# One DMA transpose per batch in place of four TensorE transposes in a gated attention and expert block on one Trainium2 core

## The reference

```python
scores = einsum('bhqd,bhkd->bhqk', heads(layernorm(x) @ Wq.T), heads(ctx @ Wk.T)) + mask
probs = softmax(scores, axis=-1)
att = merge(einsum('bhqk,bhkd->bhqd', probs, heads(ctx @ Wv.T))) @ Wo.T
x = x + tanh(g_xattn) * att
xf = layernorm(x)
w, idx = top_k(softmax(xf @ Wg + bg), 2); w = w / sum(w)
x = x + tanh(g_ffn) * sum_over_experts(comb * (relu(xf @ W1 + b1) @ W2 + b2))
```

## Time and profile before

| | us |
|---|---|
| median of 3 runs | 1155.34 (1152.26 to 1156.29) |
| the profiled execution | 1155.76 |
| its span in the profile | 1154.0 |
| PE, DVE, ACT, POOL busy in it | 1071.0, 973.1, 847.2, 793.6 |
| mean granted TensorE clock | 0.965 of full speed |

### The profile page before, as it was taken

One profiled execution on the slowest core, in us unless ns is written; L12 is line 12 of the kernel. 1 busy time (PEld: TensorE's weight loads), 2 busy tenths in 40 slices (PEclk: granted clock), 3 DMA queues, 4 the chain that ended last, 5 costly groups with the idle time before them and its releaser, 6 DMA issues.

```text
span 1154.0 us, 36397 instructions
## 1 busy us (share of the span) xinstructions
PE 1071.0 (93%) x13921; PEld 785.2 (68%) x13921; DVE 973.1 (84%) x1935; ACT 847.2 (73%) x1553; POOL 793.6 (69%) x719
## 2 busy tenths in 40 slices
PE   6889898989989899998989989899998989999986
PEld 4457576767767676776767767676676767768665
DVE  5798898988979888897988979888898987888777
ACT  4878686868767787786867767687686867878765
POOL 3768576767757677676767757677676767779853
PEclk9889899999989999998999999899999999999998
DMA  8223212212222122222212222122222212212100
GB/s 201 49 54 69 62 39 56 48 38 48 57 42 43 38 59 46 50 45 49 55 34 52 52 45 45 38 54 51 47 48 53 51 27 41 48 29 56 22 11 19
DMA packets 123163, 56.91 MB, mean 49 GB/s; under 512 B 26584, under 2 KB 122864, under 8 KB 122992
## 3 DMA queue, kind: packets, MB, share of 16 engines
q1 hardware_dynamic: 122992, 54.59, 22.4%
HBM read 16.80 MB, written 4.19 MB: 18 GB/s over the span
## 4 chain that ended last, share of the span: by engine, by line
PE 61%; DVE 17%; issue 10%; POOL 8%; ACT 3%; DMA 1%; DVEq 0%; ACTq 0%; SPq 0%; POOLq 0%
PE bank L43 18%; PE bank L44 17%; PE bank L45 17%; PE bank L315 3%; DVE x2hat L643 3%; POOL hidL L884 2%; POOL ptL L921 2%; PE bank L263 2%; PE bank L300 2%; POOL rstd L869 2%; DVE comb L857 1%; DVE picked L845 1%; ACT qH L466 1%; DVE otL L782 1%; DVE vL L734 1%
## 5 line engine op out<-in xcount | busy, mean ns | idle before, releaser
L884 POOL TENSOR_TENSOR hidL<-hid,hidH 128x512 f16<-128x512 f32 x242 | 279.7, 1169 | 19.8 <-ACT hidH L496 19.6
L921 POOL TENSOR_TENSOR ptL<-pt,ptH 128x512 f16<-128x512 f32 x128 | 148.4, 1159 | 151.7 <-ACT pt L557 151.5
L466 ACT ACTIVATE qH<-bank 128x512 f16<-128x512 f32 x256 | 153.6, 605 | 75.6 <-PE bank L45 74.7
L43 PE MATMUL bank<-w2H,hidH 128*128 128x128 f16 x1024 | 187.9, 225 | 7.1 <-DVE hidL L769 4.4
L927 POOL TENSOR_TENSOR prob<-prob,row_inv 128x512 f32<-128x512 f32 x128 | 133.8, 1045 | 84.3 <-DVE row_inv L763 84.3
L44 PE MATMUL bank<-w2L,hidH 128*128 128x128 f16 x1024 | 187.5, 225 | 0.0
L45 PE MATMUL bank<-w2H,hidL 128*128 128x128 f16 x1024 | 187.2, 225 | 0.0
L486 ACT ACTIVATE hid<-bank,b1col 128x512 f32<-128x512 f32 x256 | 181.4, 709 | 7.9 <-PE bank L45 6.4
L496 ACT ACTIVATE hidH<-bank,b1col 128x512 f16<-128x512 f32 x256 | 183.6, 717 | 0.0
L651 DVE TENSOR_TENSOR qL<-bank,qH 128x512 f16<-128x512 f32 x224 | 152.5, 681 | 27.5 <-ACT qH L466 27.4
L43 PE MATMUL bank<-ptH,vdH 128*128 128x64 f16 x1024 | 118.8, 201 | 44.1 <-DVE x L716 43.0
(11 more groups left out here) (144 smaller groups left out, 3696.0 us busy)
## 6 DMA issues: line engine op xcount, KB each, us to landing
vdH<-vH SPq DMA_DIRECT2D x256, 64.0 KB, 2.1
vdL<-vL SPq DMA_DIRECT2D x256, 64.0 KB, 2.1
x_raw<-in_x SPq DMA_DIRECT2D x16, 256.0 KB, 3.5
ctx_raw<-in_ctx SPq DMA_DIRECT2D x16, 256.0 KB, 3.5
mask_raw<-in_fside_Bx1xSxS SPq DMA_DIRECT2D x32, 128.0 KB, 2.9
out_x<-x SPq DMA_DIRECT2D x16, 256.0 KB, 2.5
qH<-in_L_xattn_Wq SPq DMA_DIRECT2D x1, 512.0 KB, 5.9
qH<-in_L_xattn_Wk SPq DMA_DIRECT2D x1, 512.0 KB, 7.9
```

Of the source, the lines that this page charges most:

```text
L43: e.matmul(dst, lhs[0], rhs[0], start=start, stop=False, skip_group_check=True)
L466: act.activation(qH[:, g % 2, 2 * j + g2, :, h2, :], bk("Q", g, h)[:, :].rearrange("p (b q) -> p b q", b=GB), ACT.Copy).then_inc(s_q_high, 1)
L884: pool.tensor_tensor(hidL[:, m % 2, c, :], hid[:, k % NR, :], hidH[:, m % 2, c, :], ALU.subtract).then_inc(s_hid_low[c], 1)
L921: pool.tensor_tensor(ptL[:, b % 2, :], pt[:, b % 2, :], ptH[:, b % 2, :], ALU.subtract).then_inc(s_pt_low, 1)
```

## The change

The four transposes of PE, both copies of ACT and the `pt` tile are gone, and with them one use of a PSUM bank per batch. Both halves are now made in the layout of `prob`: in step b+1, behind the normalization, ACT copies `prob` to `prob16[..., 0, :]` in fp16 (`s_p_high`), POOL subtracts for the low half (`s_p_low`), and SP issues one DMA transpose that turns the eight 128x128 blocks of both halves into `pt16` (`s_turned`). PV waits for the DMA. `prob16` and `pt16` have two buffers. ACT's copy stands where `ptH` and `pt` stood, but belongs to batch s-1, not s-2. POOL's subtraction moves from ahead of the normalization to behind the `hidL` of the first half.

```diff
-        pt = sb("pt", [P, 2, N])
-        ptH, ptL = (sb(f"pt{p}", [P, 2, N], F16) for p in "HL")
+        prob16 = sb("prob16", [P, 2, 2, N], F16)
+        pt16 = sb("pt16", [P, 2, 2, N // P, P], F16)
...
             def probs_values(b):
...
-                pe.wait_ge(s_pt_low, b + 1)
+                pe.wait_ge(s_turned[b % 2], 16 * (b // 2 + 1))
...
-                if within(s - 2, B):
-                    transpose_probs(s - 2)
...
-                if within(s - 2, B):
-                    b = s - 2
-                    act.wait_ge(s_pt, b + 1)
+                if within(s - 1, B):
+                    b = s - 1
+                    act.wait_ge(s_normal, b + 1)
                     if b >= 2:
-                        act.wait_ge(s_pv, b - 1)
-                    act.activation(ptH[:, b % 2, :], bk("PT", b)[:, :], ACT.Copy).then_inc(s_pt_high, 1)
-                    if b >= 2:
-                        act.wait_ge(s_pt_low, b - 1)
-                    act.activation(pt[:, b % 2, :], bk("PT", b)[:, :], ACT.Copy).then_inc(s_pt_out, 1)
+                        act.wait_ge(s_turned[b % 2], 16 * (b // 2))
+                    act.activation(prob16[:, b % 2, 0, :], prob[:, b % NPB, :, :].rearrange("p j k -> p (j k)"),
+                                   ACT.Copy).then_inc(s_p_high, 1)
                 if within(eg, GROUPS):
                     hidden_relu(eg, ei, 0)
...
-                if within(s - 2, B):
-                    b = s - 2
-                    pool.wait_ge(s_pt_high, b + 1)
-                    pool.wait_ge(s_pt_out, b + 1)
-                    pool.tensor_tensor(ptL[:, b % 2, :], pt[:, b % 2, :], ptH[:, b % 2, :],
-                                       ALU.subtract).then_inc(s_pt_low, 1)
                 if within(s - 1, B):
                     b = s - 1
                     p = prob[:, b % NPB, :, :]
...
                 if within(m, GROUPS * E):
                     hidden_low(m, 0)
+                if within(s - 1, B):
+                    b = s - 1
+                    pool.wait_ge(s_p_high, b + 1)
+                    if b >= 2:
+                        pool.wait_ge(s_turned[b % 2], 16 * (b // 2))
+                    pool.tensor_tensor(prob16[:, b % 2, 1, :], prob[:, b % NPB, :, :].rearrange("p j k -> p (j k)"),
+                                       prob16[:, b % 2, 0, :], ALU.subtract).then_inc(s_p_low, 1)
...
+                if within(s - 1, B):
+                    b = s - 1
+                    if b >= 2:
+                        sp.wait_ge(s_pv, b - 1)
+                    sp.wait_ge(s_p_low, b + 1)
+                    sp.dma_start_transpose(pt16[:, b % 2, :, :, :].rearrange("p a j q -> p (a j) q"),
+                                           prob16[:, b % 2, :, :].rearrange("p a n -> p (a n)")
+                                           ).then_inc(s_turned[b % 2], 16)
```

More of the change, by code:

```diff
@@ L143, in flamingo_block @@
         s_place = [[sem(f"placed_v{buf}{g2}") for g2 in range(2)] for buf in range(2)]
+        s_turned = [sem(f"turned_p{i}") for i in range(2)]
         s_store = [sem(f"stored{i}") for i in range(2)]
         s_wpe, s_xT, s_ctxT, s_x2T = sem("weights_pe"), sem("xT"), sem("ctxT"), sem("x2T")
-        s_q, s_v, s_scores, s_pt, s_pv, s_wo = (sem(n) for n in ("q", "v", "scores", "pt", "pv", "wo"))
+        s_q, s_v, s_scores, s_pv, s_wo = (sem(n) for n in ("q", "v", "scores", "pv", "wo"))
         s_hid, s_y, s_logitT, s_logit, s_pickT, s_b2 = (
@@ L152, in flamingo_block @@
             sem(n) for n in ("weights_high", "xT_high", "ctxT_high", "x2T_high"))
-        s_q_high, s_v_high, s_exp, s_pt_high, s_pt_out, s_o_high = (
-            sem(n) for n in ("q_high", "v_high", "exp", "pt_high", "pt_out", "o_high"))
+        s_q_high, s_v_high, s_exp, s_p_high, s_o_high = (
+            sem(n) for n in ("q_high", "v_high", "exp", "p_high", "o_high"))
         s_q_out = [sem(f"q_out{i}") for i in range(2)]
@@ L176, in flamingo_block @@
         s_q_pool = [sem(f"q_low_pool{i}") for i in range(2)]
-        s_pt_low, s_normal, s_y_add, s_before, s_above = (
-            sem(n) for n in ("pt_low", "normal", "y_add", "rank_before", "rank_add"))
+        s_p_low, s_normal, s_y_add, s_before, s_above = (
+            sem(n) for n in ("p_low", "normal", "y_add", "rank_before", "rank_add"))
         s_hid_low = [sem(f"hid_low{c}") for c in range(HC)]
@@ L229, in evicted @@
                 return [(s_shift, at[0] + 1)]
-            if kind == "PT":
-                return [(s_pt_high, at[0] + 1), (s_pt_out, at[0] + 1)]
             if kind == "PV":
@@ L307, in scores @@
                 last.then_inc(s_scores, 1)
[L309 to L316, removed]
             def probs_values(b):
@@ L327, in probs_values @@
                     lhs = [v[:, t % 2, b % 2, c // CL, :, :, c % CL].rearrange("p g d -> p (g d)") for v in (vdH, vdL)]
-                    last = three_passes(pe, bk("PV", b)[:, cols], lhs, (ptH[:, b % 2, cols], ptL[:, b % 2, cols]))
+                    pts = [pt16[:, b % 2, k, c // 2, c % 2 * S:(c % 2 + 1) * S] for k in range(2)]
+                    last = three_passes(pe, bk("PV", b)[:, cols], lhs, pts)
                 last.then_inc(s_pv, 1)
@@ L773, in _ @@
                     if s >= NPB:
-                        dve.wait_ge(s_pt, s - NPB + 1)
+                        dve.wait_ge(s_p_low, s - NPB + 1)
                     dve.tensor_tensor(prob[:, s % NPB, :, :], softmax_src(s),
```

## The result

The changed kernel takes 1402.93 us (median of 4 runs, 1401.48 to 1404.60) against 1155.82 us for the kernel before (4 runs too, one more than in the table at the top): a ratio of 1.2145, 95% interval 1.2112 to 1.2177. It is 247 us slower; the prediction was 1356 with a range of 1295 to 1430.

A forecast was written before the change was run, and what follows sets the result against it. Bound: a ring of waits through DVE, POOL and ACT, with DVE idle 2.33 us per step. From 1155.8 us, +188 for 14 groups and +12 for the first 15 steps give 1356 us, range 1295 to 1430.

The forecast's parts named there:

- The trip from row_inv to otL: From DVE's row_inv through POOL's normalization and ACT's copy, relu and otH to DVE's otL: 3.05 us.
- The shortest step: In steps with attention and experts, row_inv to row_inv can never be shorter than 8.22 us.
- The group: Eight steps with attention and experts take 82.5 us against 69.1, +13.4 each, +188 us over 14 groups.
- the wait for qH: DVE waits for ACT's next qH, 0.98 us in steps without extra DVE work; taken as 3.3 us per group.
- the ring: POOL, ACT and DVE wait on each other in a closed chain that bounds the step: 1356 us, chance 0.74.
- The first 15 steps: Steps ahead of the groups, without hidden evictions: +0.9 us each for 15 steps, rounded to +12 us.
- the early ring: The same closed chain of waits without hidden evictions: otL at 2.48 us, closing at about 5.9 us.
- The tail: The last steps, without attention, were to stay unchanged.
- The DMA transpose: SP's transpose before PV: between 3.5 and 16.8 us, taken as under 10 us and hence hidden.
- The second rival: The DMA transpose is the bound, taking its queue over 10.3 us: about 1430 to 2250 us, chance 0.14.
- third rival: PE's clock falls because PE stands still some 2.5 us per step: 1504 us, chance 0.05.
- The first rival: PE stays the bound and its 0.47 us x 128 come off: 1096 us, chance 0.05.

The follow-up runs named there:

- Runs 1: Kernel before, PE transposes kept, no DMA transpose; ACT waits before ptH for batch s-1's normalization, POOL's ptL moved behind the first hidL: 1465.65 us.
- run 3: Changed kernel with only ACT's copy of batch s-1 moved behind the hidden evictions of the same step: 1117.05 us.
- Run 8: Changed kernel with POOL's low half moved behind POOL's two expert-choice instructions, in the one step per group that has them: 1393.18 us.
- run 7: Changed kernel with POOL's normalization first in steps under 16: 1398.11 us; the same edit with ACT's copy also behind the hidden evictions: 1116.34 us.
- run 2: Changed kernel with each DMA transpose done twice, the second behind the first's completion, PV, ACT and POOL waiting for both: 1407.91 us.
- the two mended orders: The kernels of run 3, 1117.05 us, and run 6, 1108.84 us.
- run 6: Changed kernel with ACT's copy, POOL's low half and SP's transpose one step later, the transpose issued ahead of the four value placements: 1108.84 us.

## Why the prediction was right, point by point

- **The trip from row_inv to otL.** Worked out as 3.05 us, measured 3.07; DVE's wait 2.33, measured 2.27 (the 2.33 counts from when DVE could have started, the trace from the end of the subtraction), and 286 us in all for a forecast of near 300. POOL, ACT and DVE each had a duration in the trace, and their sum was good to 1%.
- **The order as the cause.** Runs 1 and 3 show it from both sides: the order alone, without the DMA, gives 1466 us; the DMA, without the order, 1117.
- **The shortest step.** No step with attention and experts was to be under 8.22 us. In the steady groups the shortest is 8.71; a step without any extra work does not occur there.
- **The group.** 82.5 us forecast, 84.5 measured on average (1056.4 / 12.5); before it was 69.0. The terms of the sum against the group from 700.04 to 784.74 (84.7 us): DVE's work 60.0 less 0.5 forecast, 61.3 measured; the waits for otH 18.6, measured 18.1; the wait for POOL's root 1.1, measured 1.1; the wait for qH 3.3, measured 1.3, with 2.4 for two waits for ACT that the sum did not have (`pickedT_L` 1.5, `x2tL` 0.9). DVE's work is the term that was mis-sized, by 1.8 us. x2hat did get shorter, from 3.77 to 2.90 us, but `above` and `same` grew by 1.5 together and xhat by 0.7 (2.30 to 2.96). Run 8 shows what it is for `same`: DVE waits for POOL inside its instruction, and 0.84 us per group come off. Over 112 steps the forecast was +188 us and the measurement +220 (193.3 + 26.8). The last 12 steps gave 26.8 us where 1.5 groups at 13.4 make 20. I had priced them like the others although eight of them have no queries. In these eight (batch 119 to 127) the kernel before takes 53.1 us, some 16 less than its average group of 69.3, and the changed one 72.1, some 13 less than its 84.8. It fits that the bound of the kernel before is PE, which loses the work of the queries, while the ring keeps more of its length; no run was made on it.
- **The first 15 steps.** +12 forecast, +22.5 measured. The step that failed was to leave POOL's query low halves out of the early ring: one stood in front of the normalization (run 7: 5.7 us of the 10.5 missing); the other 4.8 are open. Two figures of that step were off as well: 15 x 0.9 is 13.5 and not 12, and the 4.98 us from row_inv to row_inv were read from four quick steps, where all 15 take 5.96 on average (89.4 / 15).
- **The tail** was to stay as it was, and took 5.1 us more; not tried.
- **The DMA transpose.** Bounded by 3.5 and 16.8 us and taken as near the lower end; 3.1 us to landing. The second rival (0.14) is refuted by run 2. The estimate that the prediction made from the Trainium skill (VectorE: DVE Perf Modes, The three transpose paths: 1,309 ns for one block by DMA), 10.5 us for eight, is not borne out: the measurement decides, and eight blocks in one DMA land in 3.1 us. The skill's figure is for one block alone, which no run here has. The other place of the Trainium skill that I named (Advanced Engine Details and Errata, X-Bar Transpose (TRN2): as fast as ordinary DMAs) agrees with it: 256 KB of x land in 3.1 us in the changed kernel's trace too (3.5 in the trace before).
- **PE's clock** (third rival, 0.05): mean 0.936 against 0.965, 0.96 in a steady group, with PE at 76% of the span and 5% of the chain. It did not bind in the steady groups.
- **The first rival** (PE stays the bound, 1096 us) is where the two mended orders go: 1117 and 1109 us. Its price for the transposes, 0.47 us of PE per batch or 3.8 per group, fits: 3.6 and 4.0 us per group came off (69.3 to 65.7 and 65.3). What it lacked was an order in which PE is the bound. By the chain, PE is that in run 6 (65%), and in run 3 only in part (28%).

## What to carry to other kernels

When a step of a software pipeline is moved earlier by one stage, list what now waits for a result of the same step, and what stands behind that wait in each queue; one copy in the wrong place cost here 286 us, nearly five times the 60 us that the removal it served could bring. Here it paid to put the instruction that waits for other engines last in its step, behind the work that they wait for. The same question is to be asked of a queue of DMAs: which one does an engine wait for first, and what is issued ahead of it? Putting the transpose ahead of four copies that were needed later gave 37 us.

## What the runs showed of the hardware that I had not expected

- One DMA transpose of 128 x 1024 fp16 elements (256 KB) inside SBUF lands in 3.1 us (median; 3.0 to 4.7) and occupies SP for 1.27 us; two plain copies of 64 KB took SP as long (1.25 us for two). The trace counts 135,164 more packets than before, some 1,056 per transpose.

```profile
706.15 1.27 SPq L1020 DMA_TRANSPOSE pt<-prob  x1
707.52 1.25 SPq L1012 DMA_DIRECT2D vdH<-vH  x2
```

- A comparison on DVE of 128x256 fp32 elements with both inputs in SBUF took 0.41 us beside an idle POOL (run 8). It took 1.3 to 1.4 us when a POOL instruction had started just before it. POOL's instructions took 1.17 and 1.36 us in that stretch of the changed kernel:

```profile
756.85 1.17 POOL L871 TENSOR_TENSOR hidL<-hid,hidH 128x512 f16<-128x512 f32 x1 [2.45 <-ACT hidH L485]
757.97 1.36 POOL L920 TENSOR_TENSOR prob<-prob 128x512 f16<-128x512 f32 x1
```

`above` started 0.13 us behind hidL (756.98 against 756.85) and ended at 758.29, 0.27 behind it; `same` started behind the low half and ended 0.28 behind that one (759.61 against 759.33). In the kernel before, hidL stood earlier against `above`:

```profile
623.07 1.16 POOL L884 TENSOR_TENSOR hidL<-hid,hidH 128x512 f16<-128x512 f32 x1
```

```profile
623.73 0.78 DVE L833 TENSOR_TENSOR above<-logit 128x256 f32<-128x256 f32 x1
```

There `above` started 0.66 us behind hidL and took 0.78 us instead of 1.31, but its end is again 0.28 behind hidL's. In all 15 places of the changed trace where POOL overlaps them, both comparisons end 0.27 to 0.29 us behind POOL's instruction. So DVE did not run slower, it waited for the end of POOL's instruction. The Trainium skill has this rule (SBUF — State Buffer, Who interferes with whom: a DVE instruction with two SBUF inputs and a GpSimd instruction that reads SBUF exclude each other, and the one that comes second waits); by it, this trace agrees. An order that keeps POOL busy at another time therefore changes DVE's durations, and a sum that takes them from the trace of before has an error of this size, here some 1.5 us per group for these two.
